# Attention: VectorE's accumulation of an older pair's weighted values set ahead of the subtraction of the current pair's scores

## What is computed

```python
q, k, v = (cproj(Wq), cproj(Wk), cproj(Wv))          # complex, 64 per head
qr, kr = q * phase, k * phase                         # rotation by the position
E = exp(clip(-mu * |t_i - t_j|, -30, 0))
s = einsum('bihd,bjhd->bhij', qr, conj(kr)).real
maha = maximum(qn + E*E*kn - 2*E*s, 0) / V
logits = coef * log1p(maha / nu) - 0.5 * 64 * log(V)
logits = where(causal, logits, -inf)
A = softmax(logits, axis=-1)
y = concat([out.real, out.imag]) ; x = x + y @ Wo      # out = A @ v
```

## Time and profile before

| | |
|---|---|
| time, median of 3 runs | 1726.16 us (1725.77 to 1736.36) |
| the profiled execution's own time | 1732.12 us, its span 1730.3 us |
| mean granted TensorE clock | 0.993 |
| PE matmul busy | 1656.3 us (96%) |
| PE weight loads busy | 1336.5 us (77%) |
| DVE busy | 1468.9 us (85%) |
| ACT busy | 1478.6 us (85%) |
| POOL busy | 986.2 us (57%) |
| first to last `distances` (L1522), 128 of them | 261.4 to 1499.4 us |

### The profile page before, as it was taken

One profiled execution on the slowest core, in us unless ns is written; L12 is line 12 of the kernel. 1 busy time (PEld: TensorE's weight loads), 2 busy tenths in 40 slices (PEclk: granted clock), 3 DMA queues, 4 the chain that ended last, 5 costly groups with the idle time before them and its releaser, 6 DMA issues. The chain is left out here.

```text
span 1730.3 us, 30644 instructions
## 1 busy us (share of the span) xinstructions
PE 1656.3 (96%) x9664; PEld 1336.5 (77%) x9664; DVE 1468.9 (85%) x3350; ACT 1478.6 (85%) x2939; POOL 986.2 (57%) x841
## 2 busy tenths in 40 slices
PE   5999988999999999999999999999999999899998
PEld 4787766877887887788788778878877887777876
DVE  6878887899889889988998898899889989877675
ACT  6677768999999999999999999999989998766755
POOL 3554555566556556655665565656556655345565
PEclk9999999999999999999999999999999999899999
DMA  6000032222222322222222322232222222100000
GB/s 173 1 1 1 1 106 65 56 65 62 65 62 64 77 50 74 53 73 53 71 71 50 77 58 69 50 77 53 74 65 62 65 50 62 25 1 13 13 7 19
DMA packets 42993, 92.29 MB, mean 53 GB/s; under 512 B 7376, under 2 KB 19280, under 8 KB 42832
## 3 DMA queue, kind: packets, MB, share of 16 engines
q1 hardware_dynamic: 42832, 90.33, 20.6%
HBM read 17.95 MB, written 5.24 MB: 13 GB/s over the span
## 5 line engine op out<-in xcount | busy, mean ns | idle before, releaser
L1455 POOL TENSOR_TENSOR early<-early 128x1024 f32<-128x1024 f32 x127 | 302.9, 2385 | 480.5 <-PE pS L1150 256.9
L652 POOL TENSOR_TENSOR hid_lo_d<-hid_d,hid_hi_d 128x512 fp32r<-128x512 f32 x176 | 231.4, 1315 | 222.1 <-ACT hid_hi_d L557 215.5
L1345 ACT ACTIVATE early<-early,qnorm 128x128 f32<-128x128 f32 (+3 forms) x512 | 246.2, 554 | 64.8 <-DVE early L1526 64.8
L1150 PE MATMUL pS<-early 128*128 128x128 f32 (+3 forms) x1024 | 299.3, 435 | 1.5 <-PEq L105 1.5
L1328 ACT ACTIVATE early<-early,nmax 128x128 f32<-128x128 f32 (+3 forms) x512 | 281.1, 561 | 14.5 <-DVE nmax L1513 14.3
L1522 DVE SCALAR_TENSOR_TENSOR pS<-pS,ek 128x1280 f32<-128x1280 f32 x128 | 191.8, 1498 | 112.5 <-PE pS L1150 112.4
L1150 PEld LDWEIGHTS pS<-early 128*128 128x128 f32 x1024 | 165.4, 192 | 97.8 <-issue 62.6
L1463 POOL TENSOR_TENSOR ek<-early 128x128 f32<-128x128 f32 (+3 forms) x256 | 216.4, 879 | 12.2 <-ACT early L1336 11.8
L1463 POOL TENSOR_TENSOR ek<-decay,early 128x128 f32<-128x128 f32 (+3 forms) x256 | 215.2, 873 | 2.2 <-ACT early L1336 2.1
L1165 PEld LDWEIGHTS pV<-ones,early 128*128 128x128 f32 x1016 | 134.3, 193 | 61.3 <-issue 61.3
L1190 PE MATMUL pS<-ident,early 128*128 128x128 f32 x1280 | 163.9, 274 | 5.2 <-DVE early L1526 4.4
(11 more groups left out here) (387 smaller groups left out, 3957.6 us busy)
## 6 DMA issues: line engine op xcount, KB each, us to landing
early<-early SPq DMA_DIRECT2D x256, 256.0 KB, 3.6
early<-trig_d SPq DMA_DIRECT2D x64, 64.0 KB, 2.0
trig_d<-early SPq DMA_DIRECT2D x3, 1024.0 KB, 6.9
early<-in_w SPq DMA_DIRECT2D x3, 704.0 KB, 9.0
x_sb<-in_x SPq DMA_DIRECT2D x4, 512.0 KB, 8.6
early<-in_wqk SPq DMA_DIRECT2D x16, 128.0 KB, 3.5
cos<-trig_d SPq DMA_DIRECT2D x32, 64.0 KB, 2.1
sin<-trig_d SPq DMA_DIRECT2D x32, 64.0 KB, 2.0
```

The lines of the kernel that those rows point to most:

```text
L652: g.tensor_tensor(hid_lo[:, par], hid[:, par], hid_hi[:, par].bitcast(F32), ALU.subtract).then_inc(lo_done, 1)
L1150: last = pe.matmul(s.pS[:, span(I)], rot[:, I * P:(I + 1) * P], rot[:, N:N + (I + 1) * P], start=True, stop=True)
L1345: last = a.activation(u[:, span(I)], u[:, span(I)], ACT.Relu, bias=qnorm[:, r % 2, I:I + 1])
L1455: g.tensor_tensor(rot[:], by_cos[:], crossed[:], ALU.add).then_inc(S["rot_done"], 1)
```

## The change

In each step VectorE's `accumulate` of pair n-3 is called ahead of `distances` of pair n, where it was called behind `query_norms` of n+1. Nothing else is changed: the same instructions run, on the same operands, with the same waits.

```diff
                 if live(i, r):
+                    if live(i, r - 3):
+                        accumulate(i, r - 3)
                     distances(i, r)
                 if n == PAIRS - 1:
                     head_low(0)
                     head_low(1)
                 if live(i, r + 1):
                     query_norms(i, r + 1)
-                if live(i, r - 3) and n != PAIRS:
+                if live(i, r - 3) and not live(i, r) and n != PAIRS:
                     accumulate(i, r - 3)
```

## The result

| | before | after |
|---|---|---|
| median of 17 runs each | 1731.09 us (1725.77 to 1737.62) | 1736.88 us (1733.85 to 1739.38) |
| ratio | | 1.0036, 95% interval 1.0023 to 1.0049 |
| span of the profiled execution | 1730.3 us | 1737.3 us |
| its own time | 1732.12 us | 1739.09 us |
| first to last `distances` (L1522) | 261.39 to 1499.43 | 261.23 to 1510.16 |

What follows compares the result with a forecast made beforehand. The loop of waits between three nearly full engines was taken as the bound, TensorE setting plain odd steps. Odd heads +9.5, last head +0.7, collisions -1.8, tail -1.4 give +7.0 us: 1726.2 to 1733.2 us, range 1720 to 1744.

Steps and rivals of the forecast that it cites:

- The wait removed: Plain odd step: TensorE no longer waits at `weigh` for the late accumulation; alone, 9.02 us falls by 0.39 to 8.63.
- The new wait: Plain odd step: VectorE, free at 5.47 us, waits ahead of `peaks` for ScalarE's logarithms, about 0.9 us.
- Circle: `distances`, `clamp`, `turned_out`, `logs`, `peaks`, accumulations, next `distances`: 9.32 us first, 9.21 in a run, setting the plain odd step.
- Odd head: Pair 0 +0.30, pair 1 0, pairs 2 to 4 +0.69, pairs 5 to 7 +0.57, next head -0.20: +1.36 us, seven times.
- Even heads: Steps of 10.04 us stay unchanged: VectorE's idle 1.58 us takes in the accumulations' 1.03; 0 us.
- Collisions of `build_front` with GpSimd: Odd heads: GpSimd's last piece lengthens two `build_front` instructions; most of this taken as gone, -1.8 us, or 0 if none.
- the 0.66 us of room: Even heads: VectorE's idle time left per step after the accumulations fill part of 1.58 us and `peaks` starts 0.11 earlier.
- Last head and tail: Last head: three plain steps, +0.7 us. Tail: TensorE's idle 1.40 us ahead of the last pair's `weigh` goes, -1.4 us.
- VectorE's sum rules either way: Last head, pairs with `moments`: VectorE's own busy time sets the step before and after, so no change was counted.
- TensorE's gain: Rival: circle through ScalarE closes under 8.63 us, 31 plain steps gain 0.39 each; -15.3 us in all, 1711 us; chance 0.06.
- the circle close at 9.02: Rival, plain odd steps: nothing moved on balance, only collisions and tail won or neither; 1723 to 1726 us; chance 0.12.
- GpSimd did not get in the way: Rival, odd heads: GpSimd's pieces hold VectorE's reductions, 0.47 us in each of 40 steps, +18.8; 1752 us; chance 0.07.

Runs made afterwards that it cites:

- k in front: Kernel before, with the first one, two or three of four accumulations ahead of `distances`, the rest in the old place: ratios 0.9975, 0.9971, 0.9998.
- the shorter copy: Changed kernel, with ScalarE's `turned_out` copying 640 of 1280 columns in odd heads: ratio 0.9956 to the kernel before, plain odd step 8.67 us.
- the mixture: Changed kernel, but odd heads: one accumulation ahead of `distances`, three right behind; even heads: old order; last step: all four ahead. 1720.41 us, 0.9924 to the kernel before.

## Why the prediction was right, point by point

*The wait removed.* 0.39 us at `weigh`, put down to `acc_done`: shown by the run with accumulations left out, 8.63 us.

*The new wait.* `peaks` follows the logarithms by 0.31 us and starts 6.28 us after `distances`, though VectorE is done at 888.82 + 0.17 - 883.43 = 5.56 (5.47 in the prediction). Circle 9.21: measured 9.21. The runs with k in front and the shorter copy each move one piece of the circle, and where the circle is the longest the step moves with it within 0.01 us. That each piece was read from a different place of the trace of before did no harm.

*Odd head.* Predicted +1.36 us for a head with one behind it, where -0.20 of that falls in the next head's first step, and 0.26 us less for collisions, so +1.10. Measured from the positions of `distances`: the seven odd heads took 523.76 us in place of 514.07, the seven even ones behind them 1.17 less, (9.69 - 1.17) / 7 = +1.22. Pairs 2 to 4 cost 865.02 - 836.59 = 28.43 us from `distances` of 58 to that of 61, against 857.31 - 829.60 = 27.71 before: +0.72 for the +0.69 predicted. The two rows of the changed kernel:

```profile
836.59 1.49 DVE L1522 SCALAR_TENSOR_TENSOR pS<-pS,ek 128x1280 f32<-128x1280 f32 x1
...
865.02 1.48 DVE L1522 SCALAR_TENSOR_TENSOR pS<-pS,ek 128x1280 f32<-128x1280 f32 x1
```

*Even heads:* 0, shown by the run with the change there alone.

*Collisions of `build_front` with GpSimd,* taken as gone in odd heads (-1.8 us). Groups of the changed kernel, against the earlier trace rows:

```profile
L1485 DVE TENSOR_SCALAR early<-dist,early 128x1280 f32<-128x1280 f32 x7 | 6.2, 886 | 0.2
L1483 DVE COPY hp<-params 128x10 f32<-128x10 f32 x6 | 2.3, 381 | 0.0
L1483 DVE COPY early<-params 128x10 f32<-128x10 f32 x7 | 1.0, 140 | 0.0
```

They are gone in odd heads (999 to 886 ns and 285 to 140), and the seven steps that hold them are 1.9 us shorter in all, for the 1.8 predicted. They have come up in even heads (139 to 381), as `build_front` there is 1.03 us sooner against a GpSimd that is not (in pair 65 its last piece ends 5.85 us after `distances` before and 5.86 now); the 0.66 us of room hide them.

*Last head and tail.* The tail behind the last `distances` fell by 3.75 us (230.9 to 227.15). Of this the wait is 1.6 us, for the -1.4 forecast; the other 2.2 are the half clock in the tail of the kernel before, which the run with the change in even heads did not have with the same idle time. The last head took 0.6 us less in place of 0.7 more. Its plain steps cost the expected +0.69. The three steps behind them (pairs 123 to 125), put at nothing because "VectorE's sum rules either way", took 0.13 us less each, 9.62 for 9.74 in pair 124: before, `moments` reads x_sb right behind the accumulations and its first instruction came 1.15 us after theirs, where the four alone take 1.03. The last step took 9.80 for 10.72; this 0.9 is the clock again, at 0.50 for 6.8 us (1490 to 1497) in the kernel before and for 3.4 in the changed one, and the run with the change in even heads, also with 3.4, took 9.85 in the old order. Against this, the changed kernel's profile has the 3.0 us of half clock in its first pairs.

So the 7.0 us between the two profiles are: loop +8.5, first pairs +3.0 and -0.2 ahead of them, last head -0.6, tail -3.75. Without the clock it is 8.5 + 0.7 - 0.4 - 1.6 = +7.2 us. The mechanism and the sum were right; that the profiles differ by exactly the forecast figure is partly luck, since three clock effects of +3.0, -0.9 and -2.2 us nearly cancel in it.

*The rivals.* TensorE's gain does not come with four in front, since the circle is too long; it comes in the mixture. Nor does the circle close at 9.02: the gap of 0.31 us is there in full, and `logs` starts 5.26 us after `distances`, as predicted. GpSimd did not get in the way: in the changed kernel's profile no reduction of heads 1 to 14 is lengthened. In pairs 5 to 7 of the odd heads its last piece ends 5.1 to 5.7 us after `distances`, and `peaks` starts at 6.28. (Two plain steps, pairs 40 and 77, are 0.2 us longer, with VectorE idle between two reductions and GpSimd idle too; why is not shown.) But that it can be dear shows in the profile of two in front, at the end of pair 105's step:

```profile
1290.61 2.45 POOL L1455 TENSOR_TENSOR early<-early 128x1024 f32<-128x1024 f32 x1 [1.96 <-DMA early<-early]
```

```profile
1290.74 2.59 DVE L1513 CUSTOM_DVE_ANT_0 early<-early,lam,hp 128x256 f32<-128x256 f32 x1
```

GpSimd's `rotate` began 0.13 us sooner, and a reduction of 0.48 us took 2.59. The step took 12.62 us, where the same step of the other odd heads took 9.38 to 9.97, and TensorE was busy for half of 1290 to 1297 us. The granted clock of the next 8 us was 0.79:

```profile
1290.00:1297.00 7.00, 3.49 (x21) 2.42 (x20) 6.97 (x13) 3.88 (x12) 4.00 (x4) 1.00 0.26 71
1297.00:1305.00 8.00, 8.00 (x42) 6.73 (x42) 6.50 (x16) 7.88 (x16) 2.80 (x3) 0.79 0.28 69
```

By the Trainium skill, SBUF — State Buffer, section "SBUF: two separate sides", of a VectorE instruction with two SBUF inputs and a GpSimd instruction that reads SBUF, the one that starts first has the shared pair of ports for the whole instruction. The trace agrees: the addition ends at 1290.61 + 2.45 = 1293.06, and the reduction 0.27 us behind it.

*What stays open.* It is not shown what decides the length of the stretches of half clock in the first pairs and whether there is one in the tail. One profile of each run, two of the kernel before, are too few for it.

## What to carry to other kernels

When an instruction is moved on an engine, its room is not that engine's idle time but the slack of every circle of waits that passes through the new place: sum the circle piece by piece from the trace, with the gap between one engine's end and the other's start (0.31 us here) as a piece of its own. A block of several instructions need not be moved whole. Here the first quarter was worth 0.26 us a step and the last cost 0.26, and the mixture, with one in front and three right behind in the odd heads, gained 0.8% (0.5 to 1.0) where all four in front lost 0.4. And a difference in the clock between two single profiles is not an effect of the change before other profiles with the same instructions show it too.

## What the runs showed of the hardware

A wait of VectorE for ScalarE's logarithms ends 0.31 us after the logarithms' reported end, with one, two, three and four accumulations in front. A VectorE reduction of 0.48 us that starts 0.13 us behind a GpSimd addition of 2.45 us takes 2.59 us. Between executions the first 8 pairs took 84.8 to 85.7 or 88.2 us, and at 88.2 the clock was at 0.50 for 6.8 us more. In the tail, the same idle 1.40 us on TensorE stood beside a granted clock of 0.50 in two profiles and of 1.00 in a third, so it does not decide the clock alone.
